# First pass in 32-row halves with its columns of ones on chip, and a reordered layer chain, in a four-layer equivariant convolution

## The chip, the cores and the metric

The kernel runs on one core of one Trainium2 chip. The metric is the device time of one execution in microseconds, the median of several runs. Arrays are fp32 throughout; a 2048 KB transfer is 16 KB for each of the 128 partitions.

## What is computed

The input x is (1, 16, 2048, 2048). Four layers of the same form are applied:

```python
x = x + conv(_gn(x), weights, bias)     # four times
# _gn: mean and variance over groups of 2 channels and all 2048 x 2048 places
# conv: the sum of 15 basis terms; for each partition of {i-in, j-in, i-out, j-out}
#   Y += einsum(reduce X to the entry itself, its transpose, row sums, column sums,
#               diagonal, trace or total; spread it back; channels c -> o by weights[i]) / denom
# return Y + sum(bias)
```

Every term is linear in x, its transpose, its row and column sums, its diagonal, its trace and its total. So after four layers the output is one 16-to-16 channel mix of x[i,j] and x[j,i], plus a term for the row, a term for the column and a term for the diagonal. The normalisations need only second moments, which come from the Gram matrix of the channels. The kernel therefore reads x once for sums and Gram matrix, runs the four layers on 96 x 80 matrices, and reads x a second time to write the output.

## The kernel before

**First pass.** `lay_out` prepares the input on the host: x and its transpose side by side (32 "channels"), upper triangle only, in 264 tiles of 64 rows by 128 columns, the columns on the partitions. Each tile carries the columns of ones ("marks") that give row sums as extra columns of the Gram product: in groups of 8 rows there are 260 numbers, 256 of data and 4 marks. Two tiles are one transfer `early<-pairs` of 2080 KB (line 438), into a ring of 4 such slots; SyncE's queue issues a load once TensorE (`gram_done`) and VectorE (`summed`) are through with the slot's old tiles (lines 436, 437).

For each tile TensorE does 32 products (line 785), each with 64 stationary and 66 moving columns, chosen by `chunk`; a stationary or a moving operand takes every second number of a row (8 bytes apart). The fp32 product is two instructions in the trace. Alternate products go to columns 0 to 63 and 64 to 127 of the array (two "lanes" in this document). Four tiles (a quad) accumulate in one half of PSUM; ScalarE copies the sums out (line 565) and GpSimd adds them up (lines 479, 492). VectorE sums each tile over its rows into 32 numbers a partition (line 636), which GpSimd adds to `col_sum` (line 535). Between these GpSimd builds the layers' matrices, two terms a tile (lines 511 to 521).

**Between the passes.** SyncE's queue has by then issued six loads of the second pass (2048 KB each) and a half one into buffers that the first pass doesn't use, then four loads into the first pass's ring once all tiles are done (lines 447 to 450), then one into the buffer that held `spread` (line 452). Meanwhile the chain of small steps runs: row sums (line 819), means, covariance (line 840), then four layers (lines 694 to 716 on VectorE, 850 to 877 on TensorE). A layer is: centre and product with `phi` (854, 855); difference, square, product, row sum (697 to 700); group energies (862, 863); square root on ScalarE (588) and one Newton step (702 to 709); normed matrix (710, 711); four products with the layer's matrices (872 to 875); three additions (713 to 715). `link` makes VectorE wait for its own instruction's end before the next. In layer 0 the features are also transposed (868) and copied to `f2` by ScalarE (593); in layer 1 TensorE waits for that copy (line 857). `spin` issues products nobody reads. After the layers come the coefficients, the row term (888, 891) and the column term in four banks (893, copied out at 600).

**Second pass.** 128 units of two strips and one half strip; for each strip four 512-column products with the 128 x 128 `mixer` (line 912), one addition of row and column term (755, 763), and a store per unit on ScalarE's queue; strip 0 goes in two halves (743, 755; stores 607, 609), strips of the first two units one by one (612). A ring of 11 units is reloaded by SyncE's queue when a unit's stores have landed (454, 455).

Of the kernel before, what the change touches and what calls it, by code (L numbers as in the profile page):

```python
# [20 lines left out]
DATA = PAIR * SUB  # L21
EIGHT = 2 * DATA + MARKS * COLS
VW = RANGE // SUB // 2 * EIGHT
QUAD = 4
DIA_TURN = 3
# [3 lines left out]
V_SLOTS = 2 * QUAD  # L29
# [10 lines left out]
def quads(n):  # L40

    nb = n // BLK
    plain = {2 * J + e: [[(0, BLK, 2 * J + e, (J + k) % nb, False)] for k in range(1, nb // 2 + (J < nb // 2))]
             for J in range(nb) for e in range(2)}
    high, low = list(range(nb // 2)), list(range(nb // 2, nb))  # L50
    mixed = nb // 4
    couples = list(zip(high[:mixed], low[:mixed]))
    for side in (high[mixed:], low[mixed:]):
        couples += list(zip(side[0::2], side[1::2]))
    split, pure, odd = [], {}, []
    for J, K in couples:
        ranges = (2 * J, 2 * J + 1, 2 * K, 2 * K + 1)
        count = [len(plain[r]) for r in ranges]

        def left(xyz):  # L60
            x, y, z = xyz
            return (count[0] - x - y, count[1] - 3 + x, count[2] - z, count[3] - 6 + z + y)

        xyz = next(p for p in itertools.product(range(QUAD), repeat=3)
                   if min(left(p)) >= 0 and sum(k % QUAD > 0 for k in left(p)) == 1)
        x, y, z = xyz
        tri = [[(0, 64, 2 * b, b, True), (64, BLK, 2 * b + 1, b, True)] for b in (J, K)]
        rect = [(64, BLK, 2 * J, J, False), (0, 64, 2 * K + 1, K, False)]
        for special, (r, use), (s, other) in ((tri[0], (2 * J, x), (2 * J + 1, 3 - x)),
                                              (rect, (2 * J, y), (2 * K + 1, 3 - y)),  # L70
                                              (tri[1], (2 * K, z), (2 * K + 1, 3 - z))):
            split.append([special] + [plain[r].pop() for _ in range(use)] + [plain[s].pop() for _ in range(other)])
        for r in ranges:
            while len(plain[r]) >= QUAD:
                pure.setdefault(r // 2, []).append([plain[r].pop() for _ in range(QUAD)])
            if plain[r]:
                odd.append(plain[r])
    odd.sort(key=len)
    split += [odd[k] + odd[-1 - k] for k in range(len(odd) // 2)]
    last = max(pure, key=lambda b: len(pure[b]))  # L80
    return split + [g for b in pure if b != last for g in pure[b]] + pure[last], last, len(pure[last])


def pair_tiles(n):
    return [tile for group in quads(n)[0] for tile in group]


def quad_ranges(n):

    return [list(dict.fromkeys(piece[2] for tile in group for piece in tile)) for group in quads(n)[0]]  # L90
# [12 lines left out]
def lay_out(x):  # L103
# [4 lines left out]
    tiles = pair_tiles(n)  # L108
    v = np.zeros((len(tiles), BLK, RANGE // SUB // 2, EIGHT), np.float32)
    row = np.arange(RANGE)[:, None]  # L110
    first_of = (0, DATA + MARKS * COLS)
    ranges = quad_ranges(n)
    for t, tile in enumerate(tiles):
        for lo, hi, r, J, half in tile:
            at = DATA + COLS * ranges[t // QUAD].index(r)
            v[t, lo:hi, :, at:at + COLS] = 1.0
            i, j = row + r * RANGE, J * BLK + np.arange(lo, hi)[None]
            for h, a in enumerate((x, xt)):
                blk = a[:, r * RANGE:(r + 1) * RANGE, J * BLK + lo:J * BLK + hi]
                if half:  # L120
                    blk = np.where((i <= j if h == 0 else i < j)[None], blk, np.float32(0))
                blk = blk.reshape(CH, RANGE // SUB // 2, 2, SUB, hi - lo).transpose(4, 1, 2, 0, 3)
                for e in range(2):
                    at = first_of[e] + h * CH * SUB
                    v[t, lo:hi, :, at:at + CH * SUB] = blk[:, :, e].reshape(hi - lo, RANGE // SUB // 2, CH * SUB)
# [5 lines left out]
    v = v.reshape(len(tiles) // 2, 2, BLK, VW).transpose(0, 2, 1, 3)  # L131
    return np.ascontiguousarray(v).reshape(len(tiles) // 2, BLK, 2 * VW), *as_units(z.reshape(len(strips(n)), BLK, n))

# [76 lines left out]
def constants(n):  # L210
# [21 lines left out]
    def channel_spread(first, weight):  # L232
# [15 lines left out]
        "dia_scale": np.broadcast_to(np.where(f < 4 * CH, 1., -1.) / (2. * n * n), (BLK, FEATS)),  # L248
        "blocks": blocks,
        "block_scale": blocks * np.where(f < 3 * CH, 1. / n, -.5 / n),  # L250
# [3 lines left out]
        "centre": same_group * centre[r // CH] * (o < 4 * CH),  # L254
# [17 lines left out]
def build(nc, n, v, twos, half, dia, weights, biases, const_f32, twos_out, half_out, out_dia, where):  # L272
# [3 lines left out]
    sums = n // 2 // PAIR  # L276
    groups = n // SUB
    per_block = BLK // SUB
    tiles = pair_tiles(n)
    spans = quad_ranges(n)  # L280
    _, late_block, late_quads = quads(n)
    todo = strips(n)
# [9 lines left out]
    with ctx:  # L292
# [136 lines left out]
        def _(sp):  # L429
# [19 lines left out]
            for d in range(own_twos, TWOS):  # L449
                load(d)  # L450
# [11 lines left out]
        def _(pool):  # L462
# [38 lines left out]
            def matrices():  # L501
# [7 lines left out]
                for i, (o, k, _) in enumerate(step_terms):  # L509
# [3 lines left out]
                    if i % 2:  # L513
                        yield
# [444 lines left out]
```

## Time and profile before

| | us |
|---|---|
| median of 3 runs | 1932.92 |
| lowest and highest | 1931.58, 1934.33 |
| the profiled execution | 1930.29 |
| its span by the profile | 1928.5 |

| stretch | us from the start of the span |
|---|---|
| first pass (first pair landed to last product) | 10 to 674 us |
| chain between the passes | 674 to 717 us |
| second pass (first output block to last store) | 717 to 1926 us |

The engines' busy shares over the whole span (PE 81%, DVE 67%, POOL 16%, ACT 4%) mix the three stages; the views by stage are the ones to read. Of the DMA engines the profile gives the busy share and the bytes moved per time; both belong together, since engines can be busy at a lower rate.

### The profile page before, as it was taken

How to read it: one execution, taken by the hardware profiler on the slowest of the kernel's cores; microseconds unless marked ns; L12 is line 12 of the kernel's file. 1: busy time of each engine (PE TensorE's matmuls, PEld its weight loads, DVE VectorE, ACT ScalarE, POOL GpSimd, SP SyncE). 2: the span in 40 equal slices, each digit the busy share in tenths (PEclk: the TensorE clock that was granted, in tenths of full speed). 3: DMA queues.
4: the chain of work that ended last, by engine and by line, in shares of the span. 5: the costliest groups of instructions: out<-in, count | busy, mean ns of one | idle time of the engine just before them, and what ended most of it. 6: DMA issues, size and time to landing. Idle time of an engine off the chain costs nothing.

```text
span 1928.5 us, 42325 instructions
## 1 busy us (share of the span) xinstructions
PE 1564.9 (81%) x19322; PEld 969.3 (50%) x19322; DVE 1298.3 (67%) x1261; ACT 82.3 (4%) x87; POOL 313.4 (16%) x710
## 2 busy tenths in 40 slices
PE   6898888888888899999877877877777777877871
PEld 5888888888887854434333333333333333333330
DVE  6998888888898847767655554555555555555551
ACT  1011111101111110000000000000000000000000
POOL 3874444333333410000000000000000000000000
PEclk9999999999999999999999999999999999999896
DMA  9999999999999999999999999999999999999998
GB/s 396 423 419 428 429 426 430 428 428 429 427 429 428 427 423 384 431 431 428 431 430 431 431 432 430 431 431 430 430 432 430 430 432 431 429 432 431 430 431 373
DMA packets 57179, 821.27 MB, mean 426 GB/s; under 512 B 6402, under 2 KB 6530, under 8 KB 7330
## 3 DMA queue, kind: packets, MB, share of 16 engines
q1 hardware_dynamic: 37872, 551.07, 67.2%
q10 hardware_dynamic: 19250, 269.47, 32.7%
q8 instruction: 32, 0.52, 0.1%
q14 instruction: 25, 0.20, 0.0%
HBM read 551.43 MB, written 269.09 MB: 425 GB/s over the span
## 4 chain that ended last, share of the span: by engine, by line
another core or an unknown queue 47%; DMA 27%; PE 14%; issue 4%; DVE 4%; SPq 2%; ACT 0%; DVEq 0%; POOL 0%; POOLq 0%
DMA early<-pairs 23%; PE ps L912 8%; PE ps L785 4%; DVE ring_own L636 3%; DMA out<-early 3%; SPq L431 2%; DMA ring_own<-strip_in 1%; PE ps L814 1%; PE ps L922 0%; PE ps L921 0%; PE ps L893 0%; PE ps L840 0%; PE ps L804 0%; ACT shared L593 0%
## 5 line engine op out<-in xcount | busy, mean ns | idle before, releaser
L912 PE MATMUL ps<-ring_own,mixer 128*128 128x512 f32 x1348 | 631.5, 626 | 135.1 <-DMA ring_own<-strip_in 113.7
L785 PE MATMUL ps<-early 128*64 128x66 f32 x16896 | 555.4, 225 | 115.8 <-DMA early<-pairs 97.5
L636 DVE TENSOR_REDUCE ring_own<-early 128x32 f32<-128x2048 f32 x264 | 590.9, 2281 | 76.9 <-DMA early<-pairs 76.8
L785 PEld LDWEIGHTS ps<-early 128*64 128x64 f32 x16896 | 538.6, 139 | 132.5 <-DMA early<-pairs 84.3
L755 DVE SCALAR_TENSOR_TENSOR ring_own<-ps,row_sum,stage 128x512 f32<-128x512 f32 (+2 forms) x253 | 323.4, 1278 | 317.7 <-PE ps L912 317.7
L912 PEld LDWEIGHTS ps<-ring_own,mixer 128*128 128x128 f32 x1348 | 264.9, 200 | 502.2 <-issue 460.7
L912 PE MATMUL ps<-early,mixer 128*128 128x512 f32 x704 | 327.1, 621 | 75.3 <-DMA early<-strip_in 62.0
L755 DVE SCALAR_TENSOR_TENSOR early<-ps,row_sum,stage 128x1536 f32<-128x1536 f32 (+2 forms) x132 | 169.5, 1284 | 168.0 <-PE ps L912 168.0
L912 PEld LDWEIGHTS ps<-early,mixer 128*128 128x128 f32 x704 | 137.0, 199 | 265.0 <-issue 246.7
L492 POOL TENSOR_TENSOR shared<-shared,stage 128x512 f32<-128x512 f32 x132 | 167.8, 1293 | 0.0
L763 DVE SCALAR_TENSOR_TENSOR ring_own<-ps,row_sum,stage 128x508 f32<-128x508 f32 (+55 forms) x334 | 144.6, 474 | 0.0
L535 POOL TENSOR_TENSOR col_sum<-col_sum,ring_own 128x32 f32<-128x32 f32 (+1 forms) x272 | 70.3, 258 | 353.6 <-DVE ring_own L636 348.7
L565 ACT ACTIVATE stage<-ps 128x1056 f32<-128x1056 f32 x66 | 69.4, 1052 | 596.1 <-PE ps L785 587.2
L763 DVE SCALAR_TENSOR_TENSOR early<-ps,row_sum,stage 128x436 f32<-128x436 f32 (+49 forms) x174 | 75.3, 474 | 0.0
L479 POOL TENSOR_TENSOR row_sum<-row_sum,stage 128x8 f32<-128x8 f32 x188 | 34.7, 213 | 5.7 <-POOL col_sum L535 0.7
L814 PE MATMUL ps<-const 128*128 128x384 bf16 x110 | 20.4, 326 | 0.2 <-ACT shared L593 0.2
L511 POOL TENSOR_SCALAR ring_own<-ring_own,const 96x64 f32<-96x64 f32 x33 | 14.6, 442 | 3.2
L814 PEld LDWEIGHTS ps<-const 128*128 128x128 bf16 x110 | 10.3, 100 | 5.7 <-ACT shared L593 0.4
L512 POOL TENSOR_TENSOR step_m<-step_m,ring_own 96x64 f32<-96x64 f32 x33 | 10.6, 322 | 2.7
L771 DVE COPY shared<-ps 16x512 f32<-16x512 f32 x4 | 2.7, 687 | 6.9 <-PE ps L922 6.9
L520 POOL TENSOR_SCALAR ring_own<-ring_own,const 96x64 f32<-96x64 f32 x16 | 7.1, 442 | 1.6
L521 POOL TENSOR_TENSOR step_mean<-step_mean,ring_own 96x64 f32<-96x64 f32 x16 | 5.1, 320 | 1.3
(136 smaller groups left out, 108.4 us busy)
## 6 DMA issues: line engine op xcount, KB each, us to landing
early<-pairs SPq DMA_DIRECT2D x132, 2080.0 KB, 15.3
ring_own<-strip_in SPq DMA_DIRECT2D x84, 2048.0 KB, 18.3
out<-ring_own ACTq DMA_DIRECT2D x82, 2048.0 KB, 77.8
early<-strip_in SPq DMA_DIRECT2D x44, 2048.0 KB, 18.3
out<-early ACTq DMA_DIRECT2D x44, 2048.0 KB, 78.7
out<-ring_own ACTq DMA_DIRECT2D x3, 1024.0 KB, 5.7
out<-ring_own ACTq DMA_DIRECT2D x2, 512.0 KB, 6.5
const<-const_f SPq DMA_DIRECT2D x1, 798.0 KB, 26.1
```

The source lines that it names most:

```text
L431: sp.dma_start(two_buf[d % TWOS], twos[d]).then_inc(z_in[d % TWOS], 16)
L479: last = nc.gpsimd.tensor_tensor(rows[:, :, e], rows[:, :, e], got[:, :, e, k if e else WIDE + k], ALU.add)
L492: last = nc.gpsimd.tensor_tensor(total[:, :, e], total[:, :, e], got[:, :, e, at:at + WIDE], ALU.add)
L511: link(nc.gpsimd.tensor_scalar(part_w, wt[:, k], by[:, i:i + 1], None, ALU.mult))
L535: last = nc.gpsimd.tensor_tensor(col_sum[lo:hi, J], col_sum[lo:hi, J], part_sum[lo:hi, t % sums], ALU.add)
L565: nc.scalar.activation(stage[:, q % 2].rearrange("p (b m) w -> p b m w", m=BANK_REGIONS), regions(q), ACT.Copy).then_inc(gram_staged, 1)
L636: nc.vector.tensor_reduce(part_sum[:, t % sums], pairs_of(s), AX.XYZ, ALU.add).then_inc(summed, 1)
L755: ins = nc.vector.scalar_tensor_tensor(buf[:, at + done:at + done + wide * BANK].rearrange("p (b w) -> p b w", b=wide), acc[:, b:b + wide] ...
L763: ins = nc.vector.scalar_tensor_tensor(buf[:, at + done:at + done + piece], acc[:, b, off:off + piece], row_term[:, g:g + 1], col_term[:, ...
L785: last = mm(regions(parity)[lane:lane + WIDE, m // BANK_REGIONS, m % BANK_REGIONS], chunk(slot, k, False), chunk(slot, k, True), start=ope ...
L814: mm(ps[:, bank, BLK:512], moving[:, 0:BLK], moving, start=True, stop=True)
L912: last = mm(ps[:, first + at // BANK, 0:piece], mixer[:, :, :].rearrange("p a m -> p (a m)"), buf[:, at:at + piece], start=True, stop=True)
```

## The change

- The first pass has 260 tiles. A tile is two 32-row halves from neighbouring 128-row blocks, each with its own 128 columns. Two tiles are 2048 KB; the marks are no longer in the input. They are written once into the tail of each ring slot (and altered twice) by VectorE and GpSimd. Rows are innermost in a slot, so both operands of a product of the first pass now take numbers 256 bytes apart.
- VectorE's sum of a tile gives 64 numbers a partition (two halves by 32) over 32 adjacent numbers each. GpSimd adds 64 numbers a tile, and builds one term of the matrices a tile, not two. The scaled copy of the diagonal moves from VectorE to ScalarE.
- Groups of the Gram sum are 2, 2, then 4 tiles each. The diagonal's product comes one turn later.
- The four loads into the first pass's ring are issued one by one as their slots come free.
- Layers: the centring is folded into the constant matrix; copy and product are issued without a wait between; ScalarE takes the root straight from PSUM with the epsilon as its bias; the Newton step has three instructions after the reciprocal in place of four; the product for `state_t` comes first and each of the two additions signals by itself; the mean row is made once, in the last layer.
- Two of the four banks of the column term are made before the first half of strip 0, the others behind it.

```diff
-            for t in range(0, len(tiles), 2):
-                s = t % V_SLOTS
-                if t >= V_SLOTS:
-                    sp.wait_ge(gram_done, t - V_SLOTS + 2)
-                    sp.wait_ge(summed, t - V_SLOTS + 2)
-                sp.dma_start(early[:, s * VW:(s + 2) * VW], v[t // 2]).then_inc(v_in[s // 2], 16)
+            for d in range(len(tiles) // 2):
+                s = d % PAIR_SLOTS
+                if d >= PAIR_SLOTS:
+                    sp.wait_ge(gram_done, 2 * (d - PAIR_SLOTS + 1))
+                    sp.wait_ge(summed, 2 * (d - PAIR_SLOTS + 1))
+                sp.dma_start(early[:, s * PAIR_SLOT:s * PAIR_SLOT + PAIR_DATA], v[d]).then_inc(v_in[s], 16)
...
-            sp.wait_ge(gram_done, len(tiles))
-            sp.wait_ge(summed, len(tiles))
-            for d in range(own_twos, TWOS):
+            for d, pair in zip(range(own_twos, TWOS), last_pairs):
+                sp.wait_ge(gram_done, 2 * (pair + 1))
+                sp.wait_ge(summed, 2 * (pair + 1))
                 load(d)
...
-        def chunk(s, k, marked):
-
-            eight, odd = divmod(k // COLS, 2)
-            at = DATA if odd and marked else DATA + MARKS * COLS if odd else 0
-            wide = WIDE + MARKS if marked else WIDE
-            first = s * VW + eight * EIGHT + at
-            return early[:, first:first + wide * COLS].rearrange("p (e b) -> p e b", b=COLS)[:, :, k % COLS]
+        def chunk(s, e, k, marked):
+
+            got = early[:, s * PAIR_SLOT:(s + 1) * PAIR_SLOT].rearrange("p (i r) -> p i r", r=RANGE)
+            return got[:, 0:WIDE + MARKS if marked else WIDE, e * HALF + k]
+
+        def rows_of(s, e):
+
+            got = early[:, s * PAIR_SLOT:s * PAIR_SLOT + PAIR_DATA]
+            return got.rearrange("p (c h e r) -> p c h e r", h=WROWS, e=2, r=HALF)[:, :, :, e]
...
-                nc.vector.tensor_reduce(
-                    part_sum[:, t % sums],
-                    pairs_of(s), AX.XYZ, ALU.add).then_inc(summed, 1)
+                nc.vector.tensor_reduce(part_sum[:, t % sums].rearrange("p h c -> p c h"), rows_of(s, e), AX.X,
+                                        ALU.add).then_inc(summed, 1)
...
             def root(layer):
-                act.wait_ge(root_in, layer + 1)
-                nc.scalar.activation(col[:, 4:5], col[:, 3:4], ACT.Sqrt).then_inc(root_out, 1)
+                act.wait_ge(from_pe, 4 * layer + 5)
+                nc.scalar.activation(col[:, 4:5], ps[0:ROWS, 2, 0:1], ACT.Sqrt, bias=c("eps")).then_inc(root_out, 1)
...
-                dve.wait_ge(from_pe, pe_out + 1)
-                link(tt(col[:, 0:1], state[:, FEATS:], ps[0:ROWS, 0, 0:1], ALU.subtract))
-                link(tt(col[:, 1:2], col[:, 0:1], col[:, 0:1], ALU.mult))
-                link(tt(prod[:, :], state[:, 0:FEATS], ps[0:ROWS, 1, 0:FEATS], ALU.mult))
+                done = 4 * layer + 3
+                dve.wait_ge(from_pe, done + 1)
+                nc.vector.tensor_copy(col[:, 0:1], ps[0:ROWS, 0, 0:1]).then_inc(dve_own, 1)
+                tt(prod[:, :], state[:, 0:FEATS], ps[0:ROWS, 1, 0:FEATS], ALU.mult).then_inc(dve_own, 1)
+                own[0] += 2
+                dve.wait_ge(dve_own, own[0] - 1)
+                tt(col[:, 1:2], col[:, 0:1], col[:, 0:1], ALU.mult)
+                dve.wait_ge(dve_own, own[0])
                 nc.vector.tensor_reduce(col[:, 2:3], prod[:, :], AX.X, ALU.add).then_inc(to_pe, 1)
-                dve.wait_ge(from_pe, pe_out + 2)
-                nc.vector.tensor_scalar(col[:, 3:4], ps[0:ROWS, 2, 0:1], EPS, None, ALU.add).then_inc(root_in, 1)
+                dve.wait_ge(from_pe, done + 2)
                 dve.wait_ge(root_out, layer + 1)
-                link(nc.vector.reciprocal(col[:, 5:6], col[:, 4:5]))
-
-                link(tt(col[:, 2:3], col[:, 5:6], col[:, 5:6], ALU.mult))
-                link(tt(col[:, 2:3], col[:, 2:3], col[:, 3:4], ALU.mult))
-                link(nc.vector.tensor_scalar(col[:, 2:3], col[:, 2:3], -0.5, 1.5, ALU.mult, ALU.add))
-                link(tt(col[:, 5:6], col[:, 5:6], col[:, 2:3], ALU.mult))
...
+                nc.vector.reciprocal(col[:, 5:6], col[:, 4:5])
+                link(nc.vector.tensor_scalar(col[:, 3:4], ps[0:ROWS, 2, 0:1], EPS, -0.5, ALU.add, ALU.mult))
+                link(nc.vector.scalar_tensor_tensor(col[:, 7:8], col[:, 5:6], col[:, 3:4], col[:, 5:6], ALU.mult, ALU.mult))
+                link(nc.vector.scalar_tensor_tensor(col[:, 6:7], col[:, 7:8], 1.5, col[:, 5:6], ALU.add, ALU.mult))
...
+                dve.wait_ge(from_pe, done + 3)
                 tt(state_t[:, :], state_t[:, :], ps[0:FEATS, 0, 256:256 + ROWS], ALU.add).then_inc(to_pe, 1)
-                pe_in, pe_out = pe_in + 3, pe_out + 3
+                dve.wait_ge(from_pe, done + 4)
+                if layer < LAYERS - 1:
+                    tt(state[:, :], state[:, :], ps[0:ROWS, 3, 0:FEATS + 1], ALU.add).then_inc(to_pe, 1)
...
-            for b in range(banks):
+
+            def col_terms(b):
                 mm(ps[:, 4 + b, 0:BANK], coef_t[:, :, :].rearrange("f a m -> f (a m)"), f2[:, b * BANK:(b + 1) * BANK],
                    start=True, stop=True).then_inc(terms_ready, 1)
+
+            for b in range(banks // 2):
+                col_terms(b)
...
                     if p == 0 and at + BANK == n // 2:
                         last.then_inc(half_mixed, 1)
+                        for b in range(banks // 2, banks):
+                            col_terms(b)
+                        pe.wait_ge(row_term_done, 1)
```

## Rows read from the trace of the kernel before

**Rows 1.** By stage: us, busy of PE, PEld, DVE, ACT, POOL, PEclk, DMA share, GB/s
```profile
200.00:600.00 400.00, 334.88 (x10244) 324.06 (x10246) 358.37 (x161) 42.06 (x40) 158.41 (x346) 1.00 1.01 428
...
800.00:1800.00 1000.00, 808.49 (x1722) 335.04 (x1721) 569.45 (x749) 0.00 (x0) 0.00 (x0) 0.95 1.01 431
...
48.00:120.00 72.00, 63.95 (x1921) 62.92 (x1916) 66.82 (x40) 7.78 (x9) 61.22 (x157) 0.98 1.00 417
720.00:750.00 30.00, 30.00 (x71) 13.30 (x70) 21.29 (x25) 0.00 (x0) 0.00 (x0) 1.00 0.91 351
```
**Rows 2.** Chain that ended last, 205 to 235 us: start, duration, what
```profile
209.37 15.31 DMA early<-pairs
...
229.26 15.30 DMA early<-pairs
```
**Rows 3.** The page's DMA issues: name, count, size, median time to landing
```profile
early<-pairs SPq DMA_DIRECT2D x132, 2080.0 KB, 15.3
```
**Rows 4.** Timeline, first pass: start, duration, engine, line, count, idle before
```profile
58.31 17.14 PE L785 MATMUL ps<-early 128*64 128x66 f32 x547 [2.00 <-issue]
...
309.76 4.48 DVE L636 TENSOR_REDUCE ring_own<-early 128x32 f32<-128x2048 f32 x2 [0.50 <-DMA early<-pairs]
```
**Rows 5.** By line: durations in ns (min/median/max), first and last start
```profile
L888 PE MATMUL ps<-shared,coef x8: 1064/1072/1079, 709.2 to 710.1; 80*32 80x512 f32 x8
```
**Rows 6.** Timeline, 709 to 712 us: first four of L888, all eight, L893
```profile
709.21 1.08 PE L888 MATMUL ps<-shared,coef 80*32 80x512 f32 x4
...
709.21 1.98 PE L888 MATMUL ps<-shared,coef 80*32 80x512 f32 x8
...
711.43 3.70 PE L893 MATMUL ps<-shared,coef_t 80*128 80x512 f32 x8
```
**Rows 7.** By line, VectorE's sums: durations in ns
```profile
L700 DVE TENSOR_REDUCE col<-prod x4: 232/232/232, 686.8 to 703.7; 96x1 f32<-96x80 f32 x4
...
L636 DVE TENSOR_REDUCE ring_own<-early x264: 2273/2279/2289, 10.3 to 671.6; 128x32 f32<-128x2048 f32 x132
...
L673 DVE TENSOR_REDUCE feat_sum<-shared x1: 1027/1027/1027, 677.3 to 677.3; 128x32 f32<-128x512 f32 x1
```
**Rows 8.** Groups on GpSimd: count, busy us, mean ns, idle before
```profile
L511 POOL TENSOR_SCALAR ring_own<-ring_own,const 96x64 f32<-96x64 f32 x33 | 14.6, 442 | 3.2
L512 POOL TENSOR_TENSOR step_m<-step_m,ring_own 96x64 f32<-96x64 f32 x33 | 10.6, 322 | 2.7
```
**Rows 9.** Timeline of layer 1, VectorE, TensorE and ScalarE
```profile
691.12 0.24 PEld L854 LDWEIGHTS ps<-state,const 96*96 96x96 f32 x2 [0.38 <-DVE state_t L715]
...
691.73 0.15 DVE L697 TENSOR_TENSOR col<-state,ps 96x1 f32<-96x1 f32 x1 [0.66 <-PE ps L855]
691.89 0.60 PEld L814 LDWEIGHTS ps<-const 128*128 128x128 bf16 x5 [0.36 <-ACT shared L593]
...
692.37 0.23 DVE L700 TENSOR_REDUCE col<-prod 96x1 f32<-96x80 f32 x1
...
693.20 0.15 DVE L702 TENSOR_SCALAR col<-ps 96x1 f32<-96x1 f32 x1 [0.59 <-PE ps L863]
...
693.62 0.16 DVE L704 RECIPROCAL col<-col 96x1 f32<-96x1 f32 x1 [0.27 <-ACT col L588]
...
694.57 0.26 DVE L710 TENSOR_SCALAR normed<-state,col 96x80 f32<-96x80 f32 x1
...
694.97 0.33 PEld L872 LDWEIGHTS ps<-normed,step_m 96*96 96x96 f32 x2
...
696.17 0.24 DVE L713 TENSOR_TENSOR state<-state,ps 96x81 f32<-96x81 f32 x1 [1.27 <-PE ps L875]
...
696.78 0.24 PEld L854 LDWEIGHTS ps<-state,const 96*96 96x96 f32 x2 [0.38 <-DVE state_t L715]
```
**Rows 10.** Timeline, start of the second pass: stores of strips 0 and 1
```profile
718.31 0.37 ACTq L607 DMA_DIRECT2D out<-ring_own  x1
...
724.67 7.21 ACTq L612 DMA_DIRECT2D out<-ring_own  x3
```
**Rows 11.** Windows where loads run out: same columns as Rows 1
```profile
724.00:725.00 1.00, 1.00 (x4) 0.52 (x3) 0.63 (x2) 0.00 (x0) 0.00 (x0) 1.00 0.19 78
...
732.00:734.00 2.00, 2.00 (x6) 0.91 (x5) 1.67 (x1) 0.00 (x0) 0.00 (x0) 1.00 0.94 324
```

More of the change, by code:

```diff
@@ L28 @@
 BY_STRIP = 2
-V_SLOTS = 2 * QUAD
+PAIR_SLOTS = QUAD
 ROWS = 6 * CH
@@ L37, with groups_of_tiles @@
  ALL_TOTAL) = range(15)
-def quads(n):
+def groups_of_tiles(n):
     nb = n // BLK
[L48 to L81, printed above, removed]
@@ new lines, in groups_of_tiles, with column_cuts @@
+    late = parts * couples[-1][0] + parts - 2
+    pure = [([plain[r].pop() for _ in range(QUAD)], [r, r])
+            for r in [r for r in plain if r < late or r > late + 1] + [late, late + 1] for _ in range(len(plain[r]) // QUAD)]
+    for one, two in zip(mixed[1], mixed[2]):
+        out += [one, two]
+    for k, one in enumerate(mixed[3]):
+        out += [one, pure[k]]
+    return out + pure[len(mixed[3]):], late
+def column_cuts(tile, nb):
+    cuts = []
+    for lo, hi, half, _, J, _ in tile:
+        if half == 0:
+            for a, b in [(lo, 2 * lo), (2 * lo, hi)] if hi - lo > lo > 0 else [(lo, hi)]:
+                cuts += [(a, b, 0, 2, J)] if J + 1 < nb else [(a, b, 0, 1, J), (a, b, 1, 2, 0)]
+    return cuts
@@ L308, in build @@
         two_buf = [ring_own[:, 2 * s:2 * s + 2, :].rearrange("p s w -> p (s w)") for s in range(own_twos)]
-        two_buf += [early[:, 2 * (after - 1 - k) * n:2 * (after - k) * n] for k in range(after)]
+        last_pairs = range(len(tiles) // 2 - after, len(tiles) // 2)
+        two_buf += [early[:, d % PAIR_SLOTS * PAIR_SLOT:d % PAIR_SLOTS * PAIR_SLOT + 2 * n] for d in last_pairs]
         def home(u):
@@ L791, in _, with tile @@
-            quad(0, 0)
-            quad(1, 0)
+            def tile(parity, s, e, opens, closes):
+                for k in range(CHUNKS):
+                    m, lane = k // COLS, k % COLS * WIDE
+                    last = mm(regions(parity)[lane:lane + WIDE, m // BANK_REGIONS, m % BANK_REGIONS],
+                              chunk(s, e, k, False), chunk(s, e, k, True),
+                              start=opens and m % BANK_REGIONS == 0,
+                              stop=closes and m % BANK_REGIONS == BANK_REGIONS - 1)
+                last.then_inc(gram_done, 1)
@@ L826, in _ @@
             pe.wait_ge(spread_early, 1)
+            last_rows = [(b, half) for half in range(2) for b in range(nb)
+                         if (b // 2 * 2 + half) * per_block == late.start]
             for b in range(nb):
-                if b != late_block:
-                    by_rows(b)
+                for half in range(2):
+                    if (b, half) not in last_rows:
+                        by_rows(b, half)
             spin(4)
             pe.wait_ge(spread_late, 1)
-            by_rows(late_block).then_inc(from_pe, 1)
+            for b, half in last_rows:
+                last = by_rows(b, half)
+            last.then_inc(from_pe, 1)
             spin(11)
```

311 lines of the change are left out of this document (170 added, 141 removed).

## The prediction

> **What bounds the kernel now.** I read the windows by stage first. In both passes the DMA engines are busy all the time: 428 GB/s in the first pass, 431 in the second, while TensorE is busy 84% of the first pass's middle and VectorE 90% [rows 1]. The chain that ended last agrees: in the first pass it is a row of landings of `early<-pairs`, every fourth one, 19.89 us apart, so 4.97 us a pair of tiles [rows 2], each of 2080 KB, 132 of them [rows 3]. So the first pass costs what its bytes cost, with two engines not far behind: VectorE needs 4.48 us a pair [rows 4]; TensorE, where it has a backlog and runs without a gap, issues 547 instructions in 17.14 us [rows 4], 31.3 ns each, and with 128 a pair 4.01 us. The only place where the DMA engines are idle is the start of the second pass: from 720 to 750 us they move 351 GB/s [rows 1], with a hole at 724 us [rows 11]. The lost part is 30 x (431 - 351) / 431 = 5.6 us. There the 11 units of prefetch are in and stores come only as fast as the chain of the layers and the first strips let them.
>
> **Bytes.** 130 pairs in place of 132, 2048 KB in place of 2080. A pair then costs 4.97 x 2048 / 2080 = 4.90 us, and the pass 130 x 4.896 = 636.5 us in place of 132 x 4.972 = 656.4: **-19.9 us**. The constants lose 79 columns, 40 KB, -0.1 us. Rates could differ: 2048 KB loads with 16 KB a partition move in the second pass at 431 GB/s together with stores [rows 1], so I take the same rate; 1% either way would be 6 us, and half of that goes into the range.
>
> **What must stay hidden for that.** VectorE reads as many numbers per tile, 2048, now in runs of 32 in place of 4. The 80-number sum takes 232 ns, so 149 ns beside the numbers at 1.04 ns each; the tile's sum by the same count is 149 + 2133 = 2282 against 2279 measured [rows 7]: its 32 results cost nothing. With 64 results I take no more, so 4.48 us against 4.90, a reserve of 0.4 us. The marks' fills on VectorE lie ahead of the first landing at 10 us. GpSimd's term of a matrix is 442 + 322 ns [rows 8] plus waits; one a tile in place of two makes its early stretch lighter, and 51 steps of one tile end near tile 60 of 260, long before the loads that wait for `matrices_in`. The waits on the new marks stand behind four whole tiles of TensorE work (8 us) against a few short fills. ScalarE, mostly waiting, takes the diagonal's copies. From 48 to 120 us the rate is 417 GB/s in place of 428 [rows 1], 1.8 us lost while GpSimd, VectorE and TensorE catch up; I credit 0.5 of it, bounds 0 and 1.8 (the diagonal's product, one turn later, still stalls TensorE once).
>
> **TensorE is the doubtful one.** The number and shapes of instructions per tile stay (64 of 64 x 66), but both operands go from 8 to 256 bytes between numbers. No row shows that. The nearest is line 888: moving operand at 16 bytes, four lanes at once. Its first four instructions start at 709.21 us, the next four at 710.09: all eight take 1.98 us, four 1.08 [rows 5, 6], so 512 numbers in 0.88 us, 1.72 ns a number in each lane. The single-lane products of line 893, adjacent numbers, take 3.70 us for eight [rows 6] including the tail, 0.43 us each, 0.83 ns a number. Two readings are open. Either a lane that strides pays double; or the lanes share one supply. The rates of all lanes together are 512 / 427 = 1.2 numbers per ns with one lane, 66 / 31.3 = 2.1 with two lanes in the first pass [rows 4], 2048 / 880 = 2.3 with four: they level off near one number per cycle of the 2.4 GHz clock granted there, although the strides differ, 4, 8 and 16 bytes. That is what a shared supply looks like, and then stride 16 cost nothing. At the new DMA pace the first pass wants 66 x 128 / 4896 = 1.73 numbers per ns, under the 2.3 shown with one number per 16 bytes. I take this reading: cost of the stride 0, since the reserve is 4.90 against 4.01 us, 22%. The other end, double, is rival 1. Of striding weight loads no row tells.
>
> The Trainium skill has a rule against this change: "SBUF — State Buffer", section "Door 1: The DMA port swizzle", says that memory is read in lines of 16 bytes and that an access that goes to a new line each time pays a penalty, two hits a line being needed. On VectorE the trace agrees: the sum at line 673, whose numbers are 320 bytes apart, takes 1027 ns where 149 + 533 = 682 would do [rows 7], 0.67 ns a number more. For TensorE the rule gives rival 1's time; the old stride had just two hits a line.
>
> **The chain between the passes.** Layer 1 takes 691.12 to 696.78, 5.66 us [rows 9]. (a) Lines 697 to 700 take 0.87 us with three waits for their own ends; copy and product issued together leave about 0.62: -0.25. (b) From line 702 to the reciprocal 0.42 us [rows 9]; without VectorE's step -0.15. (c) Reciprocal to `normed` 0.95 us, five linked steps of 0.19; three linked steps and one not: -0.3. (d) Products and additions, 694.97 to 696.78, 1.81 us: the `state_t` product first, then two in place of three, additions of 0.24 overlapping them, and the `phi` product under the second addition: -0.9. That is 1.6 us a layer. But a wait stands in the way: in layer 1 TensorE waits for the `f2` copy until 691.85 and then spins [rows 9]. That copy comes only some 0.3 us earlier, so layer 0's gain is mostly lost there. Left: 0.3 + 1.35 + 1.6 + 1.6 = 4.8 us, bounds 3 and 6. The column term's first two banks alone ahead of strip 0 take another 1.7 us (4 of 0.43) off the first 512 KB store (718.31 now), not off the later ones (724.67) [rows 10].
>
> What that is worth: stores start 4.8 us sooner while the prefetch, 23.6 MB or 55 us after the last pair, still runs; the hole at 724 us closes, and later windows such as 732 us, busy but at 324 GB/s [rows 11], partly. Of 5.6 us I credit **4.0**, bounds 2 and 5.6. What ends last then is the DMA engines again. Issuing the ring's four loads singly is worth nothing: the queue held 13 MB, 30 us of work, when they were issued.
>
> **Sum.** 19.9 + 0.1 + 0.5 + 4.0 = 24.5 us. Against the profiled execution: span 1928.5 to 1904.0, its time 1930.3 to 1905.8. The median stands 2.6 above that execution: 1932.9 - 24.5 = **1908.4**.
>
> **Rival 1, slower: striding operands make TensorE the bound of the first pass.** If a lane pays 1.72 ns a number for its stride, an instruction takes 66 x 1.72 = 113 ns in its lane, 57 with two lanes, and with the 4 ns that it has today above 27.5 some 61 ns; 128 are 7.8 us a pair against 4.9. 130 x 2.86 = 372 us more: **2280**. It decides from 22% above today's 31.3 ns (38 ns); from 40 ns on the whole change is a loss. The rule above speaks for it, the levelling-off against. 0.16.
>
> **Rival 2, faster but less: the chain's gain does nothing.** The slow windows after 730 us have busy DMA engines, so an earlier chain may only move them. Then bytes alone, 20.0: **1913**. 0.10.
>
> **Rival 3, slower: VectorE pays per result.** Line 673's excess of 345 ns over 32 results would be 10.8 ns each; with 64 results a tile 0.69 us more, a pair 5.86 us, 125 us in all: **2033**. Line 636, with 32 results and no excess, speaks against. 0.02.
>
> **How the numbers follow.** Forecast 0.70, rival 2 0.10, rival 1 0.16, rival 3 0.02; 0.02 for a TensorE slower by just about a quarter, which ends near no change. Low end: 27.4 us gained and 1.4 of run spread, 1904, a little given: 1902. High end: bytes 17, chain 2, early -1, spread: 1916, given 2: 1918. That holds forecast and rival 2, 0.80; the slower cases are far off and stay out. A difference of 0.2% is about what can be measured: faster 0.80, same 0.02, slower 0.18.
>
> **What would show it.** Right: landings of pairs in the chain 4.90 us apart; VectorE idle 0.4 us a pair, waiting for DMA; line 785's successor still 31 to 33 ns an instruction in a backlog; a layer near 4.1 us; no window near 78 GB/s after the prefetch. Wrong: SyncE's queue waiting for TensorE in the first pass, TensorE near 100% busy and DMA share under 1 there (rival 1); a sum of a tile longer than 2.45 us (rival 3); 720 to 750 us still near 350 GB/s (rival 2); a wait for the `f2` copy over 1 us in layer 1 if (d) is larger than I think.

## The result, and the profile after

| | before | after |
|---|---|---|
| median, us | 1932.25 | 2976.52 |
| lowest and highest (4 runs each) | 1930.01, 1934.33 | 2962.39, 2992.07 |
| span of the profiled execution | 1928.5 | 2960.6 |

The ratio is 1.541 (95% interval 1.537 to 1.544). The change makes the kernel slower by more than half; 1908.4 was predicted. The page's first parts say where: the columns of part 2 are 40 slices of 74 us.

```profile
PE 2704.9 (91%) x19032; PEld 2125.1 (72%) x19032; DVE 1991.3 (67%) x1252; ACT 290.8 (10%) x89; POOL 990.8 (33%) x681
...
PE   8999999999999999999999999997777777877873
PEld 8999999999999999999999954333333333333331
...
DMA  6344344444434444444444749999999999999999
GB/s 245 142 151 162 142 170 170 155 157 173 168 142 170 157 155 170 170 170 149 166 167 170 319 191 425 430 430 431 431 431 431 431 430 431 430 431 430 431 431 395
```

The second pass, from the 25th slice on, runs at its old rate (425 to 431 GB/s, the last slice aside). The first pass fills 23 slices; before it took 664 us, 9 slices of this width. By stage, in the columns of [rows 1]:

```profile
200.00:600.00 400.00, 399.40 (x3900) 399.12 (x3900) 398.01 (x71) 71.79 (x16) 313.45 (x214) 1.00 0.43 158
...
1800.00:2800.00 1000.00, 821.45 (x1743) 340.72 (x1742) 577.39 (x753) 0.00 (x0) 0.00 (x0) 0.94 1.01 431
```

In 400 us of the first pass TensorE is busy all the time and gets through 3900 instructions in place of 10244 [rows 1]: 102.4 ns each, against 31.3 in a backlog before [rows 4]. The granted clock is full, so it is not the clock. The DMA engines move 158 GB/s. 16640 instructions at 102.4 ns are 1704 us, and that is the pass: the group's first and last start below. The chain of waits of 600 to 700 us is one piece, all TensorE. SyncE's queue, which issues a load when a slot is free, waited for VectorE's sums before (551 us in all, and 49 us for TensorE), with the sums themselves waiting for landings; now it waits above all for TensorE. The third fence below is of the kernel before, the others are of the changed one; the last two give us in total, times and the longest:

```profile
L792 PE MATMUL ps<-early x16640: 292/402/601, 10.8 to 1707.9; 128*64 128x66 f32 x199
```
```profile
599.94 100.17 PE ps L792 x904
```
```profile
SPq L437 <- DVE ring_own L636: 551.0, 125, 11.1
```
```profile
SPq L424 <- PE ps L792: 1153.7, 95, 13.7
...
SPq L423 <- DVE ring_own L647: 447.7, 48, 26.9
```

That was not all. In the groups of 200 to 600 us (mean ns of one behind the busy time) VectorE, ScalarE and GpSimd are all slower too, ScalarE's copy and GpSimd's addition among them, whose instructions the change leaves as they were (1052 and 1293 ns a piece in the kernel before):

```profile
L792 PE MATMUL ps<-early 128*64 128x66 f32 x3868 | 397.7, 407 | 0.6 <-ACT dia_cov L578 0.6
...
L647 DVE TENSOR_REDUCE ring_own<-early 128x64 f32<-128x2048 f32 x63 | 384.1, 6199 | 0.1
L479 POOL TENSOR_TENSOR shared<-shared,stage 128x512 f32<-128x512 f32 x32 | 157.2, 5110 | 0.0
...
L567 ACT ACTIVATE stage<-ps 128x1056 f32<-128x1056 f32 x15 | 71.6, 4770 | 325.1 <-PE ps L792 325.1
```

VectorE's sum of a tile takes 6.2 us, two of them 12.4 us a pair, nearly TensorE's 13.1 (128 x 102.4 ns). So from this trace alone two causes are open: TensorE's operands, or an engine that reads in a new way (VectorE) and hinders all the others.

### The profile page after: what moved, and what is told of

The parts are those of the page before. It is cut to its first block, busy times and chain, and to the rows that moved or that the text cites. A ratio compares the mean times of both kernels' runs of the same rounds, so it can differ in the third digit from the quotient of the medians.

```text
span 2960.6 us, 41755 instructions
## 1 busy us (share of the span) xinstructions
PE 2704.9 (91%) x19032; PEld 2125.1 (72%) x19032; DVE 1991.3 (67%) x1252; ACT 290.8 (10%) x89; POOL 990.8 (33%) x681
## 4 chain that ended last, share of the span: by engine, by line
PE 63%; another core or an unknown queue 31%; DMA 3%; SPq 1%; issue 0%; DVE 0%; ACT 0%; POOL 0%; DVEq 0%; POOLq 0%
PE ps L792 57%; PE ps L941 5%; DMA out<-early 2%; SPq L417 1%; DMA ring_own<-strip_in 1%; PE ps L832 0%; DMA early<-pairs 0%; PE ps L954 0%; PE ps L953 0%; PE ps L921 0%; PE ps L861 0%; PE ps L822 0%; ACT shared L597 0%; DVE ring_own L766 0%
## 5 line engine op out<-in xcount | busy, mean ns | idle before, releaser
L792 PE MATMUL ps<-early 128*64 128x66 f32 x16640 | 1694.4, 405 | 11.4 <-DMA early<-pairs 10.8
L792 PEld LDWEIGHTS ps<-early 128*64 128x64 f32 x16640 | 1694.0, 299 | 11.5 <-issue 11.5
L647 DVE TENSOR_REDUCE ring_own<-early 128x64 f32<-128x2048 f32 x260 | 1265.7, 4970 | 376.2 <-DMA early<-pairs 376.1
L479 POOL TENSOR_TENSOR shared<-shared,stage 128x512 f32<-128x512 f32 x132 | 580.2, 4561 | 0.0
L567 ACT ACTIVATE stage<-ps 128x1056 f32<-128x1056 f32 x66 | 260.4, 3945 | 1422.4 <-PE ps L792 1422.4
L519 POOL TENSOR_TENSOR col_sum<-col_sum,ring_own 128x64 f32<-128x64 f32 (+3 forms) x292 | 263.5, 903 | 180.4 <-DVE ring_own L647 154.1
L463 POOL TENSOR_TENSOR row_sum<-row_sum,stage 128x16 f32<-128x16 f32 x132 | 60.0, 454 | 535.7 <-issue 529.3
L498 POOL TENSOR_SCALAR ring_own<-ring_own,const 96x64 f32<-96x64 f32 x33 | 37.9, 1147 | 3.4 <-POOL early L535 0.2
L499 POOL TENSOR_TENSOR step_m<-step_m,ring_own 96x64 f32<-96x64 f32 x33 | 34.8, 1055 | 2.8
L506 POOL TENSOR_SCALAR ring_own<-ring_own,const 96x64 f32<-96x64 f32 x16 | 16.3, 1020 | 1.6
L586 ACT ACTIVATE ring_own<-row_sum,const 128x480 f32<-128x480 f32 x4 | 15.5, 4688 | 0.0
```

Of the source, the lines that this page charges most:

```text
L463: last = nc.gpsimd.tensor_tensor(rows, rows, got[:, :, WIDE + mark], ALU.add)
L479: last = nc.gpsimd.tensor_tensor(total, total, got[:, m:m + REGIONS // 2, 0:WIDE], ALU.add)
L498: link(nc.gpsimd.tensor_scalar(part_w, wt[:, k], by[:, i:i + 1], None, ALU.mult))
L499: link(nc.gpsimd.tensor_tensor(dst, dst, part_w, ALU.add))
L519: last = nc.gpsimd.tensor_tensor(to, to, part_sum[lo:hi, t % sums, h:end], ALU.add)
L567: nc.scalar.activation(stage[:, q % 2].rearrange("p (b m) w -> p b m w", m=BANK_REGIONS), regions(q), ACT.Copy).then_inc(gram_staged, 1)
```

## The experiments

The theory after the result: the operands' distance makes TensorE slow, and the rest of the change does what the prediction says. Its rivals: VectorE's new way of reading is what hinders everybody; and, inside the theory, only the moving operand pays; the price grows with the distance; the price is one of powers of two.

**One edit for all distances.** Everything of the change stays, bytes, turns and waits; only where a product finds its numbers in the slot differs. M is the distance in numbers of the moving operand, W that of the stationary one. In the four runs in which one operand strides and the other is adjacent the constant epsilon is raised as well, which touches nothing in the first pass. The run at 240 bytes has an edit of its own, shown at its place.

```diff
         def chunk(s, e, k, marked):
-            got = early[:, s * PAIR_SLOT:(s + 1) * PAIR_SLOT].rearrange("p (i r) -> p i r", r=RANGE)
-            return got[:, 0:WIDE + MARKS if marked else WIDE, e * HALF + k]
+            wide, step = (WIDE + MARKS, M) if marked else (WIDE, W)
+            windows = PAIR_DATA // ((WIDE + MARKS) * step) or 1
+            first = s * PAIR_SLOT + (e * HALF + k) // step % windows * (WIDE + MARKS) * step
+            return early[:, first:first + wide * step].rearrange("p (i r) -> p i r", r=step)[:, :, (e * HALF + k) % step]
```

**Both adjacent** (M = W = 1):

> The changed kernel, but each product of the first pass reads adjacent numbers (stationary 64 and moving 66 numbers in a row, 4 bytes apart) in place of numbers 256 bytes apart; same instructions, same counts, same transfers. The Gram sums are those of other numbers, so the output is another. Theory S (the 256-byte step of the operands is what costs): line 792's products go back to 31 to 33 ns each, a pair of tiles to 4.90 us, the time to 1905 to 1915 us, which also measures all the rest of the change (bytes, chain). Theory R (something else in the change, a wait on the marks, the tiles' order, the 64 results of VectorE's sum): 102 ns an instruction stays and the time stays near 2970 us.

Measured 1907.24 us (1906.23 to 1907.76; ratio 0.988, 0.986 to 0.989; before on the same chip 1930.96). Its window, its landings in the chain and its sum of a tile:

```profile
200.00:600.00 400.00, 321.27 (x10402) 309.85 (x10400) 364.47 (x164) 43.07 (x41) 161.56 (x330) 1.00 1.01 428
```
```profile
299.14 15.00 DMA early<-pairs
...
318.72 15.00 DMA early<-pairs
...
338.29 15.29 DMA early<-pairs
```
```profile
L649 DVE TENSOR_REDUCE ring_own<-early x260: 2276/2279/2292, 10.3 to 651.4; 128x64 f32<-128x2048 f32 x130
```

The pass is bound by its bytes again, a pair every 19.57 / 4 = 4.89 us, and VectorE's sum takes 2279 ns: the new way of reading costs nothing. All the loss, 1069 us, hangs on where the operands' numbers lie.

**One operand at 256 bytes, the other adjacent** (M = 64, W = 1, then M = 1, W = 64):

> The changed kernel, moving operand (66 columns) 256 bytes apart as in the change, stationary operand (64) adjacent; the epsilon constant is raised so that the roots of the meaningless sums stay real, and the output is another. If a lane pays for its moving numbers only (rival 1 as I wrote it, 1.72 ns a number): about 57 to 61 ns an instruction, 2270 us, and the third run is fast. If both operands' reads add up on one supply (130 numbers in 102 ns, 0.78 ns each): 52 ns, 2130 to 2200 us. If only the weight loads pay: 31 ns, 1910 us.

> The changed kernel, stationary operand (64 columns) 256 bytes apart, moving operand (66) adjacent; epsilon raised as before. If the moving operand alone pays: 31 to 33 ns an instruction, about 1910 us. If both add up on one supply, 0.78 ns a number: 50 ns, 2110 to 2180 us. If the weight loads alone pay: 102 ns, 2970 us.

Measured 2509.18 and 2487.04 us, one execution each; none of the accounts written down beforehand gives these. The windows, first of the moving, then of the stationary operand:

```profile
200.00:600.00 400.00, 400.00 (x5373) 400.00 (x5371) 188.45 (x85) 22.97 (x21) 100.39 (x205) 1.00 0.60 220
```
```profile
200.00:600.00 400.00, 400.00 (x5478) 400.00 (x5478) 193.89 (x87) 23.88 (x22) 104.97 (x213) 1.00 0.61 225
```

74.4 and 73.0 ns an instruction: either operand alone is enough, and both together (102.4) are more than one. The groups of the first of the two show that with one striding operand the other engines are back at their old times, or within 5% of them:

```profile
L649 DVE TENSOR_REDUCE ring_own<-early 128x64 f32<-128x2048 f32 x84 | 188.3, 2283 | 215.4 <-DMA early<-pairs 215.3
...
L569 ACT ACTIVATE stage<-ps 128x1056 f32<-128x1056 f32 x21 | 23.0, 1094 | 379.2 <-PE ps L794 379.2
```

**The change with VectorE nearly idle.** VectorE sums one row of each half:

```diff
-            return got.rearrange("p (c h e r) -> p c h e r", h=WROWS, e=2, r=HALF)[:, :, :, e]
+            return got.rearrange("p (c h e r) -> p c h e r", h=WROWS, e=2, r=HALF)[:, :, :, e, 0:1]
```

> The changed kernel with TensorE's operands as in the change, but VectorE sums only 64 of each tile's 2048 numbers (the first row of each half), so it hardly reads SBUF in the first pass. If TensorE's reads are slow by themselves: still 95 to 102 ns an instruction and about 2900 us. If it is TensorE and VectorE (and GpSimd) in each other's way: near 61 ns by the price of line 888, 2280 us, or less.

Measured 2972.82 us, 3.7 below the change, less than its runs differ among themselves.

```profile
200.00:600.00 400.00, 399.40 (x3900) 399.14 (x3899) 54.92 (x63) 54.84 (x16) 237.81 (x188) 1.00 0.43 158
```

VectorE is busy 55 of 400 us in place of 398, and TensorE issues the same 3900 instructions. So VectorE doesn't hinder TensorE. GpSimd and ScalarE stay slow with VectorE nearly idle, while with adjacent operands and VectorE at full work they were at 1188 and 1051 ns:

```profile
L479 POOL TENSOR_TENSOR shared<-shared,stage 128x512 f32<-128x512 f32 x30 | 116.9, 3996 | 0.0
L567 ACT ACTIVATE stage<-ps 128x1056 f32<-128x1056 f32 x15 | 54.6, 3640 | 342.2 <-PE ps L792 342.2
```

It is TensorE that hinders the others, and the rival with VectorE as the cause falls. No run idles GpSimd or ScalarE.

**The distance between 16 and 240 bytes, both operands** (M = W = 4, 8, 60, 16, 32). At 240 bytes the slot has room for one such window only, so the products start at 28 neighbouring places in it:

```diff
-            got = early[:, s * PAIR_SLOT:(s + 1) * PAIR_SLOT].rearrange("p (i r) -> p i r", r=RANGE)
-            return got[:, 0:WIDE + MARKS if marked else WIDE, e * HALF + k]
+            wide = WIDE + MARKS if marked else WIDE
+            first = s * PAIR_SLOT + e * HALF + k % 28
+            return early[:, first:first + wide * 60].rearrange("p (i r) -> p i r", r=60)[:, :, 0]
```

> The changed kernel, both operands of the first pass with 16 bytes between numbers (step 4) in place of 256; every number still lies in a 16-byte stretch of its own; other numbers are summed, so the output is another. Theory P (each number from a stretch of its own costs the same, however far the next one is): 102 ns an instruction, 2970 us, and ScalarE's copy of 1056 numbers near 4 us. Theory B (what costs is the distance of 256 bytes, numbers that fall on the same part of the memory): clearly less, 31 to 60 ns, 1910 to 2280 us, and the other engines' times as in the kernel before (1.05 us, 2.28 us).

> The changed kernel, both operands with 32 bytes between numbers; other numbers are summed. Theory P: as with 16, 240 and 256 bytes. Theory B: between the 16-byte and the 256-byte step, each doubling of the step up to some size costing more (half as many parts of the memory in use).

> The changed kernel, both operands with 240 bytes between numbers in place of 256: nearly as far, but no power of two; other numbers are summed. Theory P: 102 ns an instruction, 2970 us. Theory B: as fast as the 16-byte step, whatever that is, since successive numbers no longer fall on the same part.

> The changed kernel, both operands with 64 bytes between numbers; other numbers are summed. 16, 32 and 240 bytes gave 61 to 62 ns an instruction (2296 to 2305 us), 256 bytes 103 ns (2977 us). If what 256 bytes adds begins only at 256: 62 ns, 2300 us. If it grows with powers of two: between the two, with the other engines slowed too.

> The changed kernel, both operands with 128 bytes between numbers; other numbers are summed. If what 256 bytes adds begins only at 256: 62 ns an instruction, 2300 us. If it grows with powers of two from 64 or 128 bytes on: between 62 and 103 ns.

**One operand at 16 bytes, the other adjacent** (M = 4, W = 1, then M = 1, W = 4):

> The changed kernel, moving operand 16 bytes apart, stationary operand adjacent; epsilon raised so that the roots of the meaningless sums stay real. Rival 1's account (a lane pays 1.7 ns for each moving number, weight loads are hidden): 61 ns an instruction as with both operands at 16 bytes, about 2295 us. If the two operands' costs add up on one supply: clearly less, 45 to 50 ns, 2000 to 2100 us.

> The changed kernel, stationary operand 16 bytes apart, moving operand adjacent; epsilon raised. Rival 1's account: 31 to 33 ns an instruction and about 1908 us, since only moving numbers pay. If a lane's weight load pays 1.7 ns a number just the same and the slower of the two sets the pace: 61 ns, 2295 us. If the costs add up: 45 to 50 ns, 2000 to 2100 us.

All of them in one table. The times of the kernel before, the changed one and the one with both adjacent are medians of four runs, the others are one execution each. The last column is the busy time of TensorE in the window from 200 to 600 us by its instructions:

| bytes, moving / stationary | kernel | us | ns an instruction |
|---|---|---|---|
| 4 / 4 | both adjacent | 1907.24 | 30.9 (waits for bytes) |
| 8 / 8 | before | 1932.25 | 31.3 (in a backlog) |
| 16 / 4 | h1_moving4 | 2270.12 | 60.0 |
| 4 / 16 | h2_stationary4 | 2259.18 | 59.3 |
| 16 / 16 | e5_step4 | 2296.02 | 61.7 |
| 32 / 32 | e6_step8 | 2305.42 | 62.2 |
| 64 / 64 | e7_step16 | 2213.76 | 56.6 |
| 128 / 128 | e10_step32 | 2620.91 | 81.0 |
| 240 / 240 | e8_step60 | 2295.38 | 61.5 |
| 256 / 4 | e2_moving | 2509.18 | 74.4 |
| 4 / 256 | e3_stationary | 2487.04 | 73.0 |
| 256 / 256 | after | 2976.52 | 102.4 |

The windows of 16, of 240 and of 128 bytes, then that of the stationary operand alone at 16:

```profile
200.00:600.00 400.00, 400.00 (x6481) 400.00 (x6478) 225.35 (x102) 26.61 (x26) 108.30 (x220) 1.00 0.72 266
```
```profile
200.00:600.00 400.00, 400.00 (x6508) 400.00 (x6506) 227.71 (x102) 27.40 (x26) 110.42 (x224) 1.00 0.72 266
```
```profile
200.00:600.00 400.00, 399.39 (x4929) 399.25 (x4929) 170.53 (x77) 20.89 (x20) 97.05 (x200) 1.00 0.55 202
```
```profile
200.00:600.00 400.00, 400.00 (x6748) 400.00 (x6747) 235.53 (x106) 27.32 (x26) 114.76 (x234) 1.00 0.76 277
```

What follows. (1) From 8 to 16 bytes the price doubles, and from 16 to 32, and then to 240 bytes, it hardly moves: so the price doesn't grow with the distance. (2) At 16 bytes one operand alone costs 59 to 60 ns and both 61.7. The two prices don't add up, as if the slower operand set the pace, and weights pay as much as moving numbers. At 256 bytes that isn't so: 74.4 and 73.0 alone, 102.4 together. (3) 128 and 256 bytes cost more than 240. These are powers of two, 240 isn't; 16, 32 and 64 are too and don't pay more, so the extra price begins above 64 bytes. That it belongs to powers of two rests on the one distance of 240 bytes. (4) The times add up: 16640 x 61.7 ns are 1027 us in place of the 636 us that the bytes need, and 1907 + 391 = 2298 against 2296.02 measured. The expectation that each doubling from 16 bytes on costs more was wrong at 32 and at 64. Why 64 bytes is the cheapest of them and what happens at 128 and 256 stays open; no run was made between 64 and 128 bytes or above 256.

**The whole job at 8 bytes, marks on chip.** The slot is laid out in groups of two rows, 128 numbers from memory and 4 of marks between them, so that the load writes runs of 512 bytes. The edit's main piece:

```diff
-                sp.dma_start(early[:, s * PAIR_SLOT:s * PAIR_SLOT + PAIR_DATA], v[d]).then_inc(v_in[s], 16)
+                slot = early[:, s * PAIR_SLOT:(s + 1) * PAIR_SLOT].rearrange("p (g w) -> p g w", w=GROUP)
+                sp.dma_start(slot[:, :, 0:HELD], v[d].rearrange("p (g w) -> p g w", w=HELD)).then_inc(v_in[s], 16)
```

> A complete version of the change with another layout: two rows innermost, so that both operands step by 8 bytes as in the kernel before; the columns of ones stay on chip in gaps of 16 bytes, so each 2048 KB load now lands in runs of 512 bytes (32 a partition, from one 16 KB stretch of the source) and VectorE sums runs of 2 numbers. If only the operands' step matters: 31 to 33 ns an instruction, 4.90 us a pair, 1905 to 1912 us, faster than both kernels. If runs of 512 bytes cost DMA rate: under 428 GB/s in the first pass, each per cent 6.4 us, and from 3.8% on no gain over the kernel before. If VectorE pays for runs of 2 numbers: a sum over 2.28 us, and from 2.45 us on it is the bound.

Measured 2188.03 us (2187.01 to 2189.41; ratio 1.133, 1.131 to 1.135).

```profile
200.00:600.00 400.00, 263.68 (x7284) 255.62 (x7278) 254.66 (x114) 29.40 (x28) 118.67 (x241) 0.91 1.01 296
```

TensorE now waits a third of the time. The DMA engines are busy (1.01) and move 296 GB/s in place of 428: the same 2048 KB in 512-byte runs. A pair comes every 2048 KB / 296 GB/s = 7.08 us, 2.19 more than in runs of 16 KB, 285 us in all, and 1907 + 285 = 2192. Two things changed at once there, the runs' length and their places, now 528 bytes apart; which of the two costs the rate no run tells. The marks on chip can be had at 8 bytes, but not for nothing.

**The whole job at 8 bytes, marks in the input.** 260 tiles and the new chain as in the change, the slot's layout and 2080 KB a transfer as before. How a product finds its numbers:

```diff
-            got = early[:, s * PAIR_SLOT:(s + 1) * PAIR_SLOT].rearrange("p (i r) -> p i r", r=RANGE)
-            return got[:, 0:WIDE + MARKS if marked else WIDE, e * HALF + k]
+            group, odd = divmod(k // COLS, 2)
+            at = DATA if odd and marked else DATA + MARKS * COLS if odd else 0
+            wide = WIDE + MARKS if marked else WIDE
+            first = s * PAIR_SLOT + e * TILE + group * EIGHT + at
+            return early[:, first:first + wide * COLS].rearrange("p (i r) -> p i r", r=COLS)[:, :, k % COLS]
```

> A complete version: the 260 tiles and the chain of the change, but the columns of ones come with the input again, as in the kernel before 4 numbers beside every 256, so that a transfer is one run of 16.25 KB a partition (2080 KB a pair) and both operands step by 8 bytes. 130 x 2080 KB are 4.26 MB less than before, 9.9 us at 428 GB/s; with the 3.3 us that the run with adjacent operands gained beyond its bytes: 1915 to 1919 us, faster than both kernels. If the step or the length of the runs is not all that was wrong with the two layouts tried, it is slower than that.

Measured 1919.66 us (1917.15 to 1921.78; ratio 0.993, 0.991 to 0.995; before on the same chip 1932.01). By the prediction's own rate two pairs fewer are 2 x 4.97 = 9.9 us, and with the chain's 3.3 (next run) 13.2 would be gained; 12.4 were. This version does the whole job and is faster than both kernels, than the one before by 0.7%.

**The new chain alone, in the kernel before:**

```diff
-                nc.vector.tensor_scalar(col[:, 3:4], ps[0:ROWS, 2, 0:1], EPS, None, ALU.add).then_inc(root_in, 1)
...
+                nc.vector.reciprocal(col[:, 5:6], col[:, 4:5])
+                link(nc.vector.tensor_scalar(col[:, 3:4], ps[0:ROWS, 2, 0:1], EPS, -0.5, ALU.add, ALU.mult))
...
-            for b in range(banks):
...
+            for b in range(banks // 2):
+                col_terms(b)
```

> The kernel before with only the change's chain (layers, root from PSUM, order of the column term); first pass untouched. Theory of the prediction: stores start 4 to 6 us sooner and close part of the hole at the start of the second pass; 2.0 to 4.0 us off, 1926.5 to 1928.6 us. Rival 2 of the prediction (an earlier chain only moves the slow stretch): within 1 us of the kernel before.

Measured 1928.69 us (12 runs, 1926.66 to 1932.55; ratio 0.998, 0.997 to 0.999), 3.3 us gained; the interval allows 1.4 to 5.2. Its window at the start of the second pass and VectorE's first half-strips:

```profile
720.00:750.00 30.00, 30.00 (x71) 13.30 (x70) 22.51 (x28) 0.00 (x0) 0.00 (x0) 1.00 0.97 390
```
```profile
712.26 1.28 DVE L747 SCALAR_TENSOR_TENSOR ring_own<-ps,row_sum,stage 128x1024 f32<-128x1024 f32 x1 [2.80 <-PE ps L925]
715.67 1.28 DVE L760 SCALAR_TENSOR_TENSOR ring_own<-ps,row_sum,stage 128x1024 f32<-128x1024 f32 x1 [2.12 <-PE ps L925]
```

Of the loss against 431 GB/s 30 x (431 - 390) / 431 = 2.9 us is left of 5.6 [rows 1], so 2.7 us are won there. The stage now begins 2.9 us earlier; windows moved along with it (719 to 749 us before, 714.3 to 744.3 here) have 352 and 395 GB/s, 3.0 us won.

## Why the prediction was wrong, point by point

- **What failed: "TensorE is the doubtful one", cost of the stride 0.** The step took the levelling-off of numbers per nanosecond (1.2, 2.1, 2.3 with one, two and four lanes, [rows 4 to 6]) for a supply that the lanes share. With two lanes and the moving operand alone at 16 bytes the runs give 66 / 60.0 = 1.1 numbers per ns, half of the 2.3 that line 888 had with four lanes at the same distance. So nothing levelled off: each lane paid for itself, and the rates looked alike because the distance grew along with the number of lanes. One row with two things varied can't carry a reading of either. Per number of a lane the price is 2 x 60.0 / 66 = 1.82 ns with the moving operand at 16 bytes and 2 x 59.3 / 64 = 1.85 with the stationary one; line 888 had shown 1.72 [rows 5, 6].
- **Rival 1** had the mechanism and, for 16 to 240 bytes (64 and 128 aside), the price: 61 ns an instruction and 2280 us foretold, 61.5 to 62.2 ns and 2295 to 2305 us measured. It was wrong in two points: it let only the moving operand pay, where either does, and it took a row at 16 bytes for 256, where the price is 102.4 ns. The rest of the way from 2296 to 2977 us is that. The rule of the Trainium skill that the prediction named ("SBUF — State Buffer", "Door 1: The DMA port swizzle": two hits to each line of 16 bytes) is borne out in its place: 8 bytes are free, 16 are not, for both operands. It has no size, which came from line 888, and says nothing of more at 128 or 256 bytes. The 0.16 was too little for a rival for which a row at four lanes showed just the halved pace.
- **Bytes, -19.9: right.** Landings 4.89 us apart with adjacent operands (4.90 foretold), the last tile's sum starts at 651.4 in place of 671.6 [rows 7], 20.2 us earlier against 20.5 for bytes, constants and early stretch together.
- **VectorE's sum stays 2.28 us with 64 results: right** (2279 ns), so rival 3 falls.
- **The chain, 4.0 of 24.5: right in kind, 3.3 in size, which the runs can't tell from 4.0.** The second half-strip's addition comes 2.9 us earlier (718.60 before, 715.67), where 4.8 was foretold. The larger part of what is missing is layer 1: in the kernel with adjacent operands the four layers start at 665.80, 669.84, 676.39 and 680.33 us, so 4.04, 6.55 and 3.94 us, and a layer of 4.1 was foretold, with layer 0's gain lost in the wait for `f2`. That wait costs more, and the prediction's sign for it, over 1 us in layer 1, came true with 1.41: TensorE waits for ScalarE's copies until 671.21, spins for 1.42 us, and only then makes the sums for the root, for which VectorE waits 3.11 us.

```profile
668.75 2.41 ACT L599 ACTIVATE shared<-ps,const 80x512 f32<-80x512 f32 x4 [1.53 <-PE ps L893]
...
671.21 1.42 PE L834 MATMUL ps<-const 128*128 128x384 bf16 x5 [1.41 <-ACT shared L599]
...
673.51 0.16 DVE L714 RECIPROCAL col<-col 96x1 f32<-96x1 f32 x1 [3.11 <-ACT col L594]
```

  In the kernel before, VectorE's first instructions of layers 0, 2 and 3 and its first one behind the layers start at these times:

```profile
686.18 0.15 DVE L697 TENSOR_TENSOR col<-state,ps 96x1 f32<-96x1 f32 x1 [0.66 <-PE ps L855]
...
697.38 0.15 DVE L697 TENSOR_TENSOR col<-state,ps 96x1 f32<-96x1 f32 x1 [0.66 <-PE ps L855]
...
703.03 0.15 DVE L697 TENSOR_TENSOR col<-state,ps 96x1 f32<-96x1 f32 x1 [0.66 <-PE ps L855]
...
708.06 0.17 DVE L719 TENSOR_TENSOR coef<-state_t 80x16 f32<-80x16 f32 x1
```

  So layers 0 and 1 took 11.20 us and now take 10.59: 0.6 gained, where 1.65 was counted. Layer 3 went from 5.03 to 4.05 us (680.33 to 684.38), 1.0 gained in place of 1.6; layer 2 gained its 1.7. In the kernel with the new chain alone, which has the same layer times within 0.02 us, the stretch from there to the second half-strip's addition took 11.08 us in place of 10.54. Rival 2 (the chain is worth nothing) falls: its interval excludes 0.
- **The sum.** With the one failed step taken out, the kernel with adjacent operands takes 1907.24 us; 1908.4 was the forecast. Against the kernel before on the same chip (1930.96) that is 23.7 us gained where 24.5 was foretold, so part of the closeness of the two times is luck: the kernel before ran 2 us faster beside these runs than when the forecast was made. It reads other numbers than the reference asks for, so it is a measure of the terms and not a version to be had.

## What to carry to other kernels

An edit that changes how far apart an engine's operands lie is an edit of that engine's speed, weights included; when no row shows the distance, cost it by a small kernel or by the worse reading, above all when the engine has only a fifth in reserve. Before a row is read as a shared limit, look whether the rows that level off differ in one thing only. And one step that can cost 370 us or more at a chance of one in six outweighs a certain gain of 24.

## What the runs showed of the hardware that was not expected

- **Operands at 16 bytes and more.** Either operand alone at 16 bytes brings two-lane fp32 products from 31 to 59 or 60 ns; up to 240 bytes the distance adds next to nothing, 64 bytes being 8% cheaper than 16.
- **Operands at 128 and 256 bytes.** Two-lane fp32 products (64 x 66) take 61.5 ns an instruction at 240 bytes, 81.0 at 128 and 102.4 at 256; with one operand alone at 256, 73.0 to 74.4.
- **One engine's reads slow down the others.** With both operands at 256 bytes VectorE's sum goes from 2283 to 6199 ns, ScalarE's copy from 1051 to 4770 and GpSimd's addition from 1188 to 5110 (means of 200 to 600 us, adjacent operands against the change). With one operand at 256 bytes (1094 for ScalarE's copy), or both at 128 (1087), there is almost nothing of it. The Trainium skill ("SBUF — State Buffer", "SBUF: two separate sides") says that TensorE, ScalarE and VectorE's own pair of ports never wait on anyone; here ScalarE's copy of the same shape took 4.5 times as long, so the measurement decides against it for this pattern. That copy reads PSUM; ScalarE's scaled copy that reads and writes SBUF alone shows the same, with a median of 736 ns at adjacent operands and 4524 ns in the change:

```profile
L588 ACT ACTIVATE ring_own<-row_sum,const x4: 729/736/742, 644.3 to 646.2; 128x480 f32<-128x480 f32 x4
```
```profile
L586 ACT ACTIVATE ring_own<-row_sum,const x4: 3430/4524/6273, 1684.9 to 1697.0; 128x480 f32<-128x480 f32 x4
```

  That the two findings have one cause, places in memory that all these reads meet, is a guess that no run here shows.
- **Short runs in a load.** 2048 KB in runs of 512 bytes, 528 bytes apart in SBUF, moved at 296 GB/s with the DMA engines busy all the time, in runs of 16 KB at 428.
